# Attention and a mixture of experts on one core: a new slot order, the stage behind the last first scores written out, and the expert weights split on GpSimd

## The reference

```python
# x: (8, 256, 128); 16 heads of 16; window of 128 keys; 8 experts, 2 per token
qkv = x @ w_qkv.T                               # q, k, v: 8 x 16 heads x 256 x 16
att = softmax(where(j <= i and j > i - 128, q @ k.T / 4, -inf))
x = layernorm(x + (att @ v) @ w_out.T)
probs = softmax(x @ router_w); top_p, top_e = top_k(probs, 2)
y = sum over the token's two experts of top_p * (gelu(x @ w_in[e] + b_in[e]) @ w_out[e] + b_out[e])
out = layernorm(x + y)                          # (8, 256, 128)
```

## Time and profile before

| | |
|---|---|
| median of 3 runs | 197.1 us (196.51 to 197.11) |
| profiled execution, its own time | 196.5 us |
| its span, first to last instruction | 194.8 us |
| mean granted TensorE clock | 0.994 of full |
| busy: PE, DVE, ACT, POOL | 169.4, 154.8, 114.6, 84.1 us |
| slots 11 to 63 | from about 26.5 us to 110.65 us |
| slot 64 to the first second_layer | 110.65 us to 130.38 us |
| unit(0, 2) to the end of the span | 132.25 us to 194.8 us |

### The profile page before, as it was taken

One profiled execution on the slowest core, in us unless ns is written; L12 is line 12 of the kernel. 1 busy time (PEld: TensorE's weight loads), 2 busy tenths in 40 slices (PEclk: granted clock), 3 DMA queues, 4 the chain that ended last, 5 costly groups with the idle time before them and its releaser, 6 DMA issues. The chain is left out here.

```text
span 194.8 us, 6184 instructions
## 1 busy us (share of the span) xinstructions
PE 169.4 (87%) x2450; PEld 121.5 (62%) x2460; DVE 154.8 (79%) x468; ACT 114.6 (59%) x216; POOL 84.1 (43%) x157
## 2 busy tenths in 40 slices
PE   7579887988989989889999899989999979999950
PEld 3354454655656656556656544558988869999950
DVE  6985959669598698697988999635798869898793
ACT  4542056687686766876857757564353784564720
POOL 7960006556563655746738366561043002603003
PEclk9999999999999999999999999999999999999997
DMA  5589594194780882955901000000000000020011
GB/s 142 148 232 222 168 242 132 53 212 125 158 226 11 176 206 72 214 160 110 218 13 57 2 8 0 3 0 0 5 0 0 3 27 27 0 59 0 3 53 54
DMA packets 23127, 17.25 MB, mean 89 GB/s; under 512 B 1827, under 2 KB 21179, under 8 KB 23099
## 3 DMA queue, kind: packets, MB, share of 16 engines
q1 hardware_dynamic: 23099, 16.87, 35.2%
HBM read 9.35 MB, written 7.34 MB: 86 GB/s over the span
## 5 line engine op out<-in xcount | busy, mean ns | idle before, releaser
L486 ACT ACTIVATE probs<-st 128x768 f32<-128x768 f32 x59 | 47.9, 811 | 23.8 <-PE st L1067 20.6
L443 POOL TENSOR_SCALAR_AFFINE_SELECT probs<-probs 128x1024 f32<-128x1024 f32 x32 | 35.1, 1097 | 57.4 <-ACT probs L486 57.3
L713 DVE TENSOR_REDUCE max_parts<-score_banks 128x2 f32<-128x384 f32 x64 | 32.6, 550 | 4.6 <-PE score_banks L1041 4.2
L594 ACT ACTIVATE hid<-score_banks,b_in_sb 128x512 f32<-128x512 f32 x32 | 21.9, 687 | 21.0 <-PE score_banks L1173 20.9
L716 DVE TENSOR_REDUCE max_parts<-score_banks 128x4 f32<-128x512 f32 x32 | 20.6, 686 | 13.6 <-PE score_banks L1041 13.6
L1067 PE MATMUL st<-stack 51*64 51x256 bf16 (+1 forms) x472 | 21.2, 254 | 6.2 <-ACT probs L486 5.7
L1030 PE MATMUL score_banks<-edges,ident_bf 64*64 64x256 bf16 (+1 forms) x192 | 19.0, 296 | 4.5 <-DVE max_parts L713 3.4
L1089 PE MATMUL o_bank<-probs,v 128*32 128x256 f32 x256 | 20.4, 391 | 0.0
L445 POOL TENSOR_SCALAR_AFFINE_SELECT probs<-probs 128x512 f32<-128x512 f32 x32 | 20.3, 634 | 0.0
L1067 PEld LDWEIGHTS st<-stack 51*64 51x64 bf16 (+1 forms) x472 | 8.6, 104 | 18.7 <-ACT probs L486 11.8
L860 DVE SCALAR_TENSOR_TENSOR x_rows<-st,gate,x_rows 128x128 f32<-128x128 f32 x64 | 18.1, 344 | 2.4 <-PE st L1187 2.0
(11 more groups left out here) (136 smaller groups left out, 331.2 us busy)
## 6 DMA issues: line engine op xcount, KB each, us to landing
stack<-scratch SPq DMA_DIRECT2D x28, 192.0 KB, 4.0
scratch<-parts SPq DMA_DIRECT2D x16, 192.0 KB, 4.0
scratch<-parts SPq DMA_DIRECT2D x24, 128.0 KB, 3.8
x_rows<-x SPq DMA_DIRECT2D x4, 256.0 KB, 5.6
out<-y_sb SPq DMA_DIRECT2D x8, 128.0 KB, 1.8
x_t_sb<-x_t SPq DMA_DIRECT2D x3, 256.0 KB, 4.8
w_in_sb<-w_in SPq DMA_DIRECT2D x1, 512.0 KB, 5.8
w_out_sb<-w_out SPq DMA_DIRECT2D x1, 512.0 KB, 7.9
```

What stands on the lines that cost most here:

```text
L443: pool.affine_select(out=own, in_=own, compare_op=ALU.is_ge, fill=0.0, base=0, pattern=[[0, 2], [0, 4], [1, P]], channel_multiplier=-1).th ...
L486: nc.scalar.activation(probs[g][:, :, two, :].rearrange("p k j c -> p j k c"), pair_banks(PAIRS * b + p)[:, :, 0:3 * P].rearrange("p j (k ...
L594: nc.scalar.activation(hid[e % 2][:, :], hid_bank[e % 2], ACT.Gelu_apprx_tanh, bias=b_in_sb[:, e:e + 1]).then_inc(gelu_done, 1)
L713: nc.vector.tensor_reduce(top[:, 1, r, pair:pair + 2], bank[:, 0:384].rearrange("p (h c) -> p h c", h=2), X_AXIS, ALU.max, negate=True).th ...
```

## The change

The slots of several pieces are changed, and with them the order of the pieces within a slot on TensorE, VectorE and ScalarE: the first scores now stand ahead of the turned scores in a slot, and the output, attention, x1 and logits of an item come one or two slots earlier. The two misc banks swap some of their users (turn_output to misc0, turn_attention and turn_x1 to misc1, except that the last item's x1 uses misc0), and the waits on them follow. The slot loops end with slot 63; what lay in slots 64 to 74 is written out for each engine, without idle products, and first_layer(0, 0) stands between pieces of item 7. The split of w_in goes from VectorE (two instructions) to GpSimd (16 of 128x128, two each in slots 46, 48, ... 60), behind a semaphore of its own for w_in's load.

```diff
-TURN_MAX, VALUES, S2, PV = 8, 12, 11, 15
-COPY_O, TURN_O, TURN_ATTN, PROJECT_OUT, TURN_X1, LOGITS = 22, 23, 25, 26, 30, 31
-PROJECT_QK, STACK = -14, -8
+TURN_MAX, VALUES, S2, PV = 8, 10, 11, 15
+COPY_O, TURN_O, TURN_ATTN, PROJECT_OUT, TURN_X1, LOGITS, SPLIT_X1 = 21, 22, 23, 24, 28, 30, 34
+PROJECT_QK, SUBTRACT, STACK = -14, -12, -8
+WEIGHT_SLOTS = (46, 48, 50, 52, 54, 56, 58, 60)
...
# GpSimd
+            def split_weights(e):
+                pool.wait_ge(w_in_loaded, 16)
+                pool.tensor_copy(w_in_hi[:, e, :], w_in_sb[:, e, :]).then_inc(w_hi_done, 1)
+                pool.wait_ge(w_hi_done, e + 1)
+                pool.tensor_tensor(w_in_lo[:, e, :], w_in_sb[:, e, :], w_in_hi[:, e, :].bitcast(F32), ALU.subtract).then_inc(w_lo_done, 1)
-                b = batch_at(slot, PROJECT_OUT + 1)
+                b = batch_at(slot, PROJECT_OUT + 2)
                 if b is not None:
                     first_deviation(b)
+                if slot in WEIGHT_SLOTS:
+                    split_weights(WEIGHT_SLOTS.index(slot))
+            for g in range(2, QUADS):
+                mask_probs(late, g)
+            first_deviation(late - 1)
+            for g in range(QUADS):
+                mask_probs(last, g)
+            first_deviation(late)
...
# ScalarE, order in a slot behind the exponential: copy_max, take_top, pad_v (slot VALUES + 1),
# take_middle (SUBTRACT), copy_x1 (TURN_X1 + 1), copy_output, copy_logits, copy_attention
+            copy_max(last)
+            exponentials(late, 5)
+            exponentials(late, 6)
+            exponentials(late, 7)
+            pad_v(last)
+            route_exponentials(EARLY, 1)
+            act.wait_ge(moe_w_loaded, 16 * 2)
+            exponentials(last, 0)
+            exponentials(last, 1)
+            copy_output(late)
...
+            exponentials(last, 5)
+            copy_attention(late)
+            exponentials(last, 6)
+            exponentials(last, 7)
             gelu(0, 0)
+            copy_x1(late - 1)
             gelu(0, 1)
+            copy_logits(late - 1)
...
# VectorE, order in a slot: split_x1, take_maxima, take_low, normalise, split_max, first_residual,
# first_stats and first_moments, first_norm
-                if slot == LAST_S1 + 2:
-                    split_weights()
+            route_shift(EARLY, B // 2 - 1)
+            split_x1(late - 2)
+            first_residual(late - 1)
+            first_stats(late - 1)
+            first_moments(late - 1)
+            choose(EARLY, 1, 0)
+            choose(EARLY, 1, 1)
+            first_norm(late - 1)
+            normalise(late)
+            choose(EARLY, 1, 2)
+            choose(EARLY, 1, 3)
+            first_residual(late)
+            first_stats(late)
+            first_moments(late)
+            first_norm(late)
+            split_x1(late - 1)
             add_expert(0, 0)
...
# TensorE
-                if slot > LAST_S1 + 1 and slot < LAST_S2 - 1:
-                    keep_warm(2, hid_bank[0])
-                if slot == LAST_S2 - 1:
-                    pe.wait_ge(w_lo_done, 1)
-                    first_layer(0, 0)
-            weigh_values(B - 1, QUADS - 2)
+            turn_max(last)
+            turned_scores(late, 5)
+            project_out(late - 1)
+            turned_scores(late, 6)
+            turned_scores(late, 7)
+            weigh_values(late, 1)
+            project_v(last)
+            weigh_values(late, 2)
+            turned_scores(last, 0)
+            turned_scores(last, 1)
+            weigh_values(late, 3)
+            turned_scores(last, 2)
+            turned_scores(last, 3)
+            pe.wait_ge(w_lo_done, NX)
+            first_layer(0, 0)
+            turn_output(late)
+            turned_scores(last, 4)
+            weigh_values(last, 0)
+            turned_scores(last, 5)
+            turn_attention(late)
+            turned_scores(last, 6)
+            turned_scores(last, 7)
+            weigh_values(last, 1)
+            project_out(late)
+            weigh_values(last, 2)
             first_layer(0, 1)
+            turn_x1(late - 1)
+            pe.wait_ge(moe_w_loaded, 16 * 2)
             second_layer(0, 0)
-            weigh_values(B - 1, QUADS - 1)
+            route_logits(late - 1)
+            weigh_values(last, 3)
             unit(0, 2)
```

More of the change, by code:

```diff
@@ L451, in _ @@
             pool.wait_ge(half_ready, 1)
-            for slot in range(LAST_S2 + 2):
+            for slot in range(LAST_S1 + 1):
                 n = quad_at(slot + PV - S2 - 2)
@@ L574, in _ @@
                 take_even(n)
-            for slot in range(LAST_S2 + 1):
+            for slot in range(LAST_S1 + 1):
                 n = pair_at(slot)
@@ L821, in _ @@
                 take_odd(n)
-            for slot in range(LAST_S2 + 1):
-                b = batch_at(slot, TURN_O + 1)
+            for slot in range(LAST_S1 + 1):
+                b = batch_at(slot, SPLIT_X1)
+                if b is not None:
+                    split_x1(b)
+                n = jobs_at(slot)
+                if n is not None:
+                    take_maxima(*n)
+                b = batch_at(slot, SUBTRACT + 1)
+                if b is not None:
+                    take_low(b)
+                b = batch_at(slot, TURN_O)
                 if b is not None:
                     normalise(b)
+                b = batch_at(slot, TURN_MAX - 1)
+                if b is not None:
+                    split_max(b)
+                b = batch_at(slot, PROJECT_OUT)
+                if b is not None:
+                    first_residual(b)
                 b = batch_at(slot, PROJECT_OUT + 1)
@@ L1226, in _ @@
             pe.wait_ge(consts_ready, 7)
-            for slot in range(LAST_S2 + 1):
+            for slot in range(LAST_S1 + 1):
+                n = jobs_at(slot)
+                if n is not None:
+                    scores(*n)
                 n = pair_at(slot)
@@ L1233, in _ @@
                     keep_warm(2)
-                n = jobs_at(slot)
-                if n is not None:
-                    scores(*n)
                 b = batch_at(slot, TURN_MAX)
@@ L1240, in _ @@
                     turn_max(b)
-                b = batch_at(slot, TURN_ATTN)
-                if b is not None:
-                    if b == 0:
-                        pe.wait_ge(out_w_loaded, 16)
-                    turn_attention(b)
                 b = batch_at(slot, PROJECT_OUT)
@@ L1262, in _ @@
                     project_v(b)
+                b = batch_at(slot, SUBTRACT)
+                if b is not None:
+                    subtract_top(b)
                 b = batch_at(slot, TURN_X1)
@@ L1265, in _ @@
                     turn_x1(b)
-                b = batch_at(slot, TURN_O)
-                if b is not None:
-                    turn_output(b)
                 b = batch_at(slot, LOGITS)
@@ L1273, in _ @@
                     route_logits(b)
+                b = batch_at(slot, TURN_O)
+                if b is not None:
+                    turn_output(b)
                 n = quad_at(slot)
```

126 lines of the change are left out of this document (56 added, 70 removed).

## The result

The kernel after takes 188.5 us (median of 4 runs, 187.38 to 190.73) against 197.08; the ratio is 0.9553, with a 95% interval of 0.9527 to 0.958: 4.5% faster. The forecast was 188.4 us. The ratio leaves out one of the four runs, 190.73 us, in which the granted clock was lowest (0.964 of full, against 0.979 to 0.995).

A forecast was written before the change was run, and what follows sets the result against it. TensorE, working in order and nearly always busy, was taken as the bound. Terms -2.9 - 1.3 - 0.5 + 0.4 - 4.1 = -8.4 took 196.5 to 188.1 us, with a run-median allowance 188.4; range 185.0 to 194.5.

The forecast's parts named there:

- Items 3 to 5: Slot loop: most of TensorE's waits go, an item takes 12.4 us instead of 13.37, -2.9 us for the three.
- The chain copy_output, turn_output, normalise, turn_attention: Slots 5 to 7: its first three pieces take about 2.4 us against 2.7 us of other TensorE work; fits by 0.3.
- the 0.36 and 0.31: TensorE's two waits per item, in us, for the exponential of the pair before; claimed to go.
- The 0.73: TensorE's wait per item, in us, for VectorE's maxima, put down to take_low and first_norm in slots 4 and 5.
- the 1.40 us: All of TensorE's standing in an item of 13.37 us; 0.4 us was forecast to be left.
- Items 6 and 7: Slot loop without a coming projection: 11.8 us an item instead of 12.46, with the maxima's DMA showing; -1.3 us for two.
- Items 0 to 2: Start of the slot loop: -0.5 us from item 2's waits, +0.4 because item 5's turn_attention falls ahead of slot 64.
- GpSimd's split at no cost: Slots 46 to 60: 6 us of split on GpSimd, hold-ups of VectorE included, counted as 0; upper bound 6 us.
- Behind slot 63: From slot 64 to unit(0, 2): idle products of 4.2 us go, ScalarE's chain becomes the longer; -4.1 us.
- the idle products cost nothing: Rival, behind slot 63: they stood where TensorE waits anyway, stage ends as before, 192.2 us; chance 0.13.
- The clock: Rival: TensorE's clock falls behind slot 63 without the idle products, 194 us; chance 0.03.
- Slower: Rival: TensorE stands for late pieces from weigh_values to turn_attention in slots 5 to 7, near 200 us; chance 0.07.

The follow-up runs named there:

- b_scores_first: The kernel before with one swap in TensorE's slot, the first scores ahead of the turned scores: 215.25 us, ratio 1.0872 to the kernel before.
- a_turned_first: The kernel after with turned scores and idle products again ahead of the first scores on TensorE: 188.47 us, ratio 0.9579 to the kernel before.
- b_norm_behind: The kernel before with first_norm behind the maxima of its slot on VectorE: 196.11 us, ratio 0.9963 to the kernel before.
- a_no_split: The kernel after without the split of w_in, both weight parts filled with zeros at the start: 188.6 us, ratio 0.9587 to the kernel before.
- b_gp_split: The kernel before with the split of w_in on GpSimd in slots 46 to 60, none on VectorE: 201.86 us, ratio 1.0246.
- a_idle: The kernel after with the sixteen idle products put back, all ahead of first_layer(0, 0): 192.07 us, ratio 0.9748 to the kernel before.
- b_no_idle: The kernel before without the sixteen idle products in slots 65 to 72: 198.65 us, ratio 1.0092 to the kernel before.
- a_spread: The kernel after with w_in loaded in slot 28 and split in slots 36 to 54: 188.35 us, ratio 0.9568 to the kernel before.

## Why the prediction was right

The sum was right to 0.1 us at the median, and to 0.8 us for the profiled execution (196.5 to 187.4, 9.1 gained where 8.4 were forecast). That closeness is in part luck. The terms were off by -1.0, +1.3, +0.2 and -1.2 us, which nearly cancel, and the median of 188.5 lies between runs that kept their clock better (187.38 and 187.89 us) and two with a lower mean clock (189.11 and 190.73 us at 0.979 and 0.964). Two of the reasons given do not hold.

*Items 3 to 5*: forecast -2.9, measured -3.9. The 0.4 us left over for new waits was too careful: one of 0.24 to 0.30 us an item. The chain copy_output, turn_output, normalise, turn_attention, which was said to fit by 0.3 us, fits. But "the 0.36 and 0.31 go because the first scores now stand between" is wrong as a cause. The swap alone makes an item longer by 1 us (b_scores_first), and taking it back in the new order brings waits of at most 0.22 us in items 3 to 5 and the same 12.1 us an item (a_turned_first). The 0.73 was traced to the right instruction, but moving that alone only exchanges it for 0.60 (b_norm_behind). So the 1.40 us go only when several pieces are moved together; which of the others is needed was not tried apart.

*Items 6 and 7*: forecast -1.3, measured 0. This step failed, and the traces show by what. First, the start was misread: 12.46 us is the distance of VectorE's maxima, while TensorE's slots of item 6 are 12.16 us apart, so 0.3 us of item 6 were never there to gain. Second, the wait for the DMA of the maxima was foreseen as 0.5 us, and it is 0.72 and 0.54 in the kernel after and 0.8 in the four variants whose item 6 is undisturbed. The DMA takes the same 3.0 us, but it is issued 0.34 us later in the item, because the exponential ahead of copy_max on ScalarE now waits for turned scores that stand behind the first scores; with the swap taken back copy_max is as early as before (a_turned_first). In the kernel after and the five variants that show this wait in item 6, the stretch up to it is 4.86 to 4.89 us long, as long as in items 3 to 5 (4.86 to 4.91), where the projection fills it: the wait stands in the projection's place. Third, item 7 of the kernel after has a wait of 0.63 us for first_norm and one of 0.26 for the split maxima, and item 6 one of 0.24 for a mask. My theory after the result, that GpSimd's split caused all this, fell with a_no_split. The split has 0.1 to 0.7 us of item 6; without it the DMA still holds the item at 12.1.

*Items 0 to 2*: forecast -0.5 + 0.4 = -0.1, measured +0.1 (item 3 starts at 46.05 and before at 45.94).

*GpSimd's split at no cost*: right in size for the whole, wrong in kind. It takes 0.29 and 0.46 us an instruction, where 0.31 and 0.42 were read from the earlier trace rows. In the new order the times don't show its cost, the traces 0.1 to 0.7 us in item 6; in the order of before it costs 1.7 us in item 6 at full clock (b_gp_split). The prediction had counted the hold-ups at 0.3 us an item, "on an engine that has about 1 us to spare". What that left out is where the instruction that is held up stands: first_norm is ahead of the maxima in the order of before, and ahead of turn_x1 in the new one.

*Behind slot 63*: forecast -4.1, measured -5.3. By its own steps the chain of ScalarE would end at 14.7 us, 0.5 was given back on top, and it ended at 13.9: from 106.87 on ScalarE's eleven exponentials take 817 ns each, where 0.85 was counted, with only 1.1 us of idle time before them in all. Why its small copies fit better than stepped was not followed further. "Gone are 4.2 us of idle products" holds only with the written-out order: there they cost 3.4 us (a_idle), and in the order of before nothing, at least up to turn_x1 (b_no_idle). The rival *the idle products cost nothing* is thus true of that part of the kernel before and false of the kernel after. What the products had covered there, above all 2.16 us for first_norm, had to go first, by the written-out order. No run has the written-out stage with the old slots, or the new slots with the old stage, so that the shares of the two in the 9.1 us are read from the traces and not from an experiment.

*The clock* was given 0.03. In the profiled run it stayed at 1.00 until the last product. In two of the other three runs the mean clock was lower. Their traces were not kept, but those of the variants, where it falls at 15 and behind 30 us, point to the start of the slot loop and not to the stage behind slot 63 that the rival meant. In three of the four single changes it fell in the profiled run, and made the loss larger than the waits alone.

*Slower*: the price of this rival holds a slip. By its own formula, 7 x (s - 0.4) = 8.4, the standing that decides against the change is 1.6 us an item, not 2.6. TensorE stood for 0.3 us in each of items 3 to 5, for 1.0 in item 6 and for 1.4 in item 7, and none of it for the chain that this rival names.

## What to carry to other kernels

A wait of an engine that works its list in order can move to the next late producer when one piece is moved, as 0.73 us became 0.60 in b_norm_behind; before counting a wait as a gain, ask what is due next. The same holds for work: where a projection left, the wait for a DMA took its place. Measure the length of a piece on the engine whose time is counted, not on another one. Filler work beside a wait is free until the wait is gone. Judge a single step of such a change by its own trace and not by its time alone, since its loss may be the clock's and not the order's.

## What the runs showed of the hardware

The granted clock of TensorE has two levels in these runs, 1.00 (2.4 GHz) and 0.50 (1.2 GHz), and fell in the middle of dense work. In b_no_idle TensorE did nothing for most of 2 us (120 to 122), took up work again, and the clock fell between 123 and 124 and was back at 1.00 at 131. The first half of weigh_values took 0.45 us ahead of the fall (its start at 110.98, the next at 111.43) and 0.83 behind it (123.47 to 124.30). In a_spread it fell at 15 us, behind a stretch from 12 to 15 in which TensorE was busy for 0.12, 0.63 and 0.66 of each us; the kernel after had 0.61, 0.39 and 0.32 there in its profiled run and kept 1.00. So a sparse stretch stood ahead of these falls but is not always followed by one, and the same kernel differs from run to run: the kernel before had a mean clock of 0.987 to 0.996 in the 34 runs beside the experiments and 0.9 us of scatter, the kernel after 187.38, 187.89, 189.11 and 190.73 us at 0.987, 0.995, 0.979 and 0.964.

VectorE's first_norm takes longer beside GpSimd's work. Its two instructions took 0.88 us in all in items 3 to 5 of the kernel before. In the kernel after they stand beside a mask and took 1.44 us, with no split near, on the timelines of VectorE and GpSimd:

```profile
75.52 1.44 DVE L811 TENSOR_SCALAR x_rows<-resid,moments,rstd 128x128 f32<-128x128 f32 x2
```

```profile
75.20 1.09 POOL L456 TENSOR_SCALAR_AFFINE_SELECT probs<-probs 128x1024 f32<-128x1024 f32 x1
```

a_no_split, without any split, has 1.44 us as well. Beside split and mask they took 1.66 us (item 7 of the kernel after) and 1.82 (b_gp_split), the longest single one 1.13 and 1.25 us. So the new wait for first_norm in items 3 to 5 comes with its new place beside the masks, and the split adds to it only later. The Trainium skill, page "SBUF — State Buffer", section "Who interferes with whom", tells of a pair of SBUF ports that the two share, locked by one at a time; the traces agree in kind.

The DMA that carries the maxima from SBUF to SBUF (two issues) took 3.0 us from the end of ScalarE's copy to the turned scores that need it, in item 6 of both kernels (87.55 to 90.53 before, 84.09 to 87.12 after).
